# A recurrent gated network on one core: output gate's tanh apart, one agent row block on VectorE, history in single passes, new order on all engines

## What is computed

```python
def step(carry, xy):
    st, err, gs, mem, h1, c1, h2, c2 = carry
    encoded = tanh(xt @ We + st @ Ue + be)                       # 24 values
    new_state = tanh(einsum('bd,cds->bcs', xt, Wx) + einsum('bs,cst->bct', st, Ws) + bk)   # 8 candidates of 32
    mem = concatenate([[encoded, err], mem[:, :-1]])             # the last 20 entries of 25
    a = relu(mem.reshape(b, -1) @ enc_w1 + enc_b1)               # 64
    agent_in = relu(a @ enc_w2 + enc_b2)                         # 16
    h1, c1 = lstm_cell(agent_in, h1, c1)
    h2, c2 = lstm_cell(h1, h2, c2)
    gate = softmax(h2 @ gate_w + gate_b)                         # 8
    theta = clamp01(mean(abs(mem[:, :10, -1])) * 2.5)
    gate = gate * theta + gs * (1 - theta)
    st = einsum('bc,bcs->bs', gate, new_state)
    pred = clamp01(st[:, -1]);  err = pred - yt
```

## Time and profile before

| what | value |
|---|---|
| median of 3 runs | 5656.33 us (5656.32 to 5656.89) |
| profiled execution: span | 5654.1 us |
| instructions | 184300 |
| phases | 512, of 10.93 us each in the middle of the run |
| VectorE busy in the window of one phase, 2799.12 to 2810.05 us | 9.08 us |
| ScalarE busy in it | 7.48 us |
| TensorE busy in it (recorded, with the tails of matmuls) | 10.63 us |

### The profile page before, as it was taken

One profiled execution on the slowest core, in us unless ns is written; L12 is line 12 of the kernel. 1 busy time (PEld: TensorE's weight loads), 2 busy tenths in 40 slices (PEclk: granted clock), 3 DMA queues, 4 the chain that ended last, 5 costly groups with the idle time before them and its releaser, 6 DMA issues.

```text
span 5654.1 us, 184300 instructions
## 1 busy us (share of the span) xinstructions
PE 5444.6 (96%) x67584; PEld 3397.7 (60%) x67584; DVE 4678.1 (83%) x12841; ACT 3830.9 (68%) x9217; POOL 1646.7 (29%) x3589
## 2 busy tenths in 40 slices
PE   7999999999999999999999999999999999999998
PEld 4666666666666666666666666666666666666665
DVE  7888888888888888888888888888888888888887
ACT  5666666666666666666666666666666666666665
POOL 2222222222222222222222222222222222222222
PEclk9999999999999999999999999999999999999999
DMA  2111111111111111111111111111111111111111
GB/s 66 28 29 30 28 31 28 31 28 31 28 31 28 31 28 28 31 28 31 28 31 28 31 28 31 28 29 30 28 31 28 31 28 31 28 31 28 31 28 39
DMA packets 299286, 172.38 MB, mean 30 GB/s; under 512 B 156734, under 2 KB 263882, under 8 KB 298714
## 3 DMA queue, kind: packets, MB, share of 16 engines
q1 hardware_dynamic: 293568, 159.42, 10.8%
q10 hardware_dynamic: 5146, 3.66, 0.2%
HBM read 74.65 MB, written 2.10 MB: 14 GB/s over the span
## 4 chain that ended last, share of the span: by engine, by line
PE 69%; ACT 15%; DVE 12%; issue 4%; DMA 0%; POOL 0%; ACTq 0%; POOLq 0%; DVEq 0%
PE chain L412 17%; PE a_ps L374 10%; PE cand_ps L343 8%; PE cand_ps L334 8%; ACT a_sb L523 6%; PE chain L399 6%; PE a_ps L363 6%; ACT gates L548 5%; DVE cell_in L708 5%; DVE added L694 4%; PE chain L308 4%; PE a_ps L385 4%; PE chain L429 4%; PE cand_ps L329 3%; ACT tanh_c L554 3%
## 5 line engine op out<-in xcount | busy, mean ns | idle before, releaser
L363 PE MATMUL a_ps<-hist,w_hist 125*64 125x512 f16 x12288 | 1700.2, 381 | 24.9 <-DMA w_hist<-enc_table 24.9
L785 DVE TENSOR_REDUCE state<-mixed 128x64 f32<-128x512 f32 x2048 | 1352.6, 681 | 34.1 <-POOL mixed L873 0.7
L541 ACT ACTIVATE cand<-cand_ps 128x512 f32<-128x512 f32 x2048 | 1154.6, 590 | 184.8 <-PE cand_ps L343 184.8
L412 PE MATMUL chain<-cell_in,cell_w 128*64 128x128 f32 x16384 | 1092.8, 276 | 0.7 <-ACT cell_in L531 0.5
L412 PEld LDWEIGHTS chain<-cell_in,cell_w 128*64 128x64 f32 x16384 | 888.3, 136 | 288.2 <-ACT cell_in L531 181.5
L900 POOL TENSOR_TENSOR err_ring<-pred_now,ys 128x8 f32 x512 | 128.6, 251 | 3106.0 <-DVE pred_now L792 3106.0
L548 ACT ACTIVATE gates<-chain 128x512 f32<-128x512 f32 x1024 | 611.4, 597 | 619.8 <-PE chain L412 619.8
L363 PEld LDWEIGHTS a_ps<-hist,w_hist 125*64 125x64 f16 x12288 | 658.6, 110 | 447.2 <-issue 26.0
L554 ACT ACTIVATE tanh_c<-gates 128x128 f32<-128x128 f32 x1024 | 316.7, 309 | 690.0 <-DVE gates L700 690.0
L694 DVE SCALAR_TENSOR_TENSOR added<-gates 128x256 f32<-128x256 f32 x1024 | 435.5, 425 | 419.4 <-ACT gates L548 419.4
L708 DVE SCALAR_TENSOR_TENSOR cell_in<-gates,tanh_c 64x128 f32<-64x128 f32 x2048 | 588.0, 287 | 159.4 <-ACT tanh_c L554 145.6
(11 more groups left out here) (74 smaller groups left out, 6660.7 us busy)
## 6 DMA issues: line engine op xcount, KB each, us to landing
x_sb<-in_x_l SPq DMA_DIRECT2D x260, 256.0 KB, 2.8
hist<-entry_parts SPq DMA_DIRECT2D x2048, 25.0 KB
w_hist<-enc_table SPq DMA_DIRECT2D x258, 128.0 KB, 2.4
y_rows<-in_y_l SPq DMA_DIRECT2D x260, 8.0 KB
ys<-in_y ACTq DMA_DIRECT2D x1, 2048.0 KB, 16.3
preds_out<-preds SPq DMA_DIRECT2D x1, 2048.0 KB, 8.1
cand<-in_encoder ACTq DMA_DIRECT2D x1, 640.0 KB, 3.8
cell_w<-in_cell ACTq DMA_DIRECT2D x2, 256.0 KB, 4.8
```

The costliest lines, as they stand in the source:

```text
L363: nc.tensor.matmul(a_ps[g][ENC * half:ENC * half + ENC, :], w_hist[0:HROWS, w_slot(u), kk, wp, :], hist[0:HROWS, xp, k, at:at + 512], star ...
L412: last = nc.tensor.matmul(chain[g][rows, P * r:P * r + P], cell_w[c][:, hf, r, :], cell_in[c][:, g, hf, :], start=False, stop=True, skip_g ...
L541: ins = nc.scalar.activation(cand[:, g, q // 2, :, q % 2, :, :].rearrange("p h s c -> p h (s c)"), cand_ps[q][:, :].rearrange("p (h k) -> ...
L785: V.tensor_reduce(state[:, g, hf, 2 * pair:2 * pair + 2, :], mixed[:, pair, hf, :, :, :], AX, ALU.add)\
```

## The change

- The tanh of a cell's gates is cut in two: columns 128 to 511 (the three gates that the cell's value needs) and then the output gate alone, with a semaphore of its own, `q_out_gate`.
- The agent input's two instructions are shared out: ScalarE keeps one half of the rows, VectorE takes the other (`agent_input` there, semaphore `q_in_high`).
- The history product is called in pieces of one or two passes (`PIECES`), which are put between other work.
- The candidates' bias matmul leaves its place beside the candidates and goes behind the newest entry's product.
- `q_sum` and the pool's product get a semaphore for each half or tile, and waits that were together are put where each is needed; the two copies of the hidden value are separated.
- All four engines have a new order within the phase. A semaphore count is shifted where a phase now sees an item earlier or later.

```diff
-SUMS = 2
-CAND_ORDER = (2, 1, 3, 0)
-MIX_ORDER = (1, 0)
+CAND_ORDER = (1, 0, 2, 3)
+FIRST_HALF = (0, 0)
+PIECES = ((0, 0), (1, 0), (0, 1))
...
             def state_transpose(item, hf):
                 g, n, u = item
-                pe.wait_ge(q_sum[hf], SUMS * n)
+                for pair in range(2):
+                    pe.wait_ge(q_sum[hf][pair], n)
...
+            def history(item, kk, first=0, end=len(PIECES)):
                 g, n, u = item
                 k = HT - 1 - kk
-                for t, (wp, xp) in enumerate(((0, 0), (1, 0), (0, 1))):
+                for t in range(first, end):
+                    wp, xp = PIECES[t]
...
             def phase(items, extra):                      # tensor
                 new, cur, old = items
+                if old:
+                    history(old, 3, 2, 3)
+                    encoder1_now(old)
+                    candidates_bias(old)
+                if cur:
+                    history(cur, 0, 1, 2)
+                if old:
+                    bias_of_cell(old, 0)
+                    encoder2(old)
+                if cur:
+                    history(cur, 0, 2, 3)
+                    history(cur, 1, 0, 2)
+                if old:
+                    cell_gates(old, 0)
+                    candidates_x(old)
+                    candidates_s(old)
+                if cur:
+                    encoded_x(cur, extra)
+                if old:
+                    bias_of_cell(old, 1)
+                    cell_gates(old, 1)
+                if cur:
+                    history(cur, 1, 2, 3)
+                    state_transpose(cur, 0)
+                    state_transpose(cur, 1)
+                    history(cur, 2, 0, 2)
                 if old:
                     logit_bias(old)
+                if new:
+                    history_waits(new, extra)
+                    history(new, 0, 0, 1)
+                if cur:
+                    encoded_s(cur)
+                    history(cur, 2, 2, 3)
+                    history(cur, 3, 0, 2)
                 if old:
                     gate_logits(old)
...
             def cell_tanhs(item, c):
                 g, n, u = item
                 act.wait_ge(q_cps[c], n)
-                nc.scalar.activation(gates[c][:, g, 0:4, :].rearrange("p r b -> p (r b)"), chain[g][:, :],
+                nc.scalar.activation(gates[c][:, g, 1:4, :].rearrange("p r b -> p (r b)"), chain[g][:, P:4 * P],
                                      ACT.Tanh).then_inc(q_gates[c], 1)
+
+            def cell_tanh_out(item, c):
+                g, n, u = item
+                nc.scalar.activation(gates[c][:, g, 0, :], chain[g][:, 0:P], ACT.Tanh).then_inc(q_out_gate[c], 1)
...
             def phase(items, extra):                      # scalar
...
                 if new:
                     encoded(new)
                 if cur:
                     candidates(cur, 3)
+                    exponentials(cur)
                 if new:
                     entry_high(new)
                     encoder1(new)
                 if cur:
+                    next_hidden(cur, 0)
+                if new:
+                    agent_input(new, 0)
+                    cell_tanhs(new, 0)
+                if cur:
+                    next_hidden(cur, 1)
+                if new:
+                    cell_tanh_out(new, 0)
+                    value_tanh(new, 0)
+                    candidates(new, 1)
+                    candidates(new, 0)
+                    candidates(new, 2)
+                    cell_tanhs(new, 1)
+                    cell_tanh_out(new, 1)
...
+            def agent_input(item, hf):                    # vector
+                g, n, u = item
+                rows = AGENT_ROWS[hf]
+                dve.wait_ge(q_inps, n)
+                V.tensor_scalar(cell_in[0][rows, g, hf, :], a_ps[g][rows, 0:P], enc2_bias[rows, 0:1], 0.0,
+                                ALU.add, ALU.max).then_inc(q_in_high, 1)
...
             def phase(items, extra):                      # vector
...
+                    mix(cur, 0)
+                if new:
+                    agent_input(new, 1)
+                if cur:
                     mix(cur, 1)
+                    mix_sum(cur, 0, 0)
                 if new:
                     cell_terms(new, 0)
                     cell_value(new, 0)
                 if cur:
+                    mix_sum(cur, 1, 1)
+                if new:
+                    new_hidden(new, 0, 0)
+                    new_hidden(new, 0, 1)
+                    error_sum(new)
+                if cur:
+                    mix_sum(cur, 0, 1)
+                    mix_sum(cur, 1, 0)
+                    prediction(cur)
+                if new:
+                    cell_terms(new, 1)
```

More of the change, by code:

```diff
@@ L136, in recurrent_kernel @@
                                     "inps", "in", "candps"))
-        q_keptfrom, q_mulpool = (sem(f"q_{n}") for n in ("keptfrom", "mulpool"))
+        q_keptfrom = sem("q_keptfrom")
+        q_mulpool = [sem(f"q_mulpool{q}") for q in range(2)]
         q_cand = [sem(f"q_cand{q}") for q in range(Q)]
@@ L147, in recurrent_kernel @@
                                     "ring", "predout"))
-        q_sum = [sem(f"q_sum{hf}") for hf in range(HF)]
+        q_out_gate = [sem(f"q_out_gate{c}") for c in range(2)]
+        q_in_high = sem("q_in_high")
+        q_sum = [[sem(f"q_sum{hf}_{pair}") for pair in range(2)] for hf in range(HF)]
         block = ctx.enter_context(nc.Block())
@@ L298, in x_wait, with encoded_x @@
                     pe.wait_ge(s_x[x_slot(u)], extra[0][u] if extra else 16)
-            def encoded_x(item, before, extra):
+            def encoded_x(item, extra):
                 g, n, u = item
                 x_wait(item, extra)
-                if before:
-                    for pair in MIX_ORDER:
-                        pe.wait_ge(q_mul[pair], before[1] + GROUPS if pair == MIX_ORDER[1] else before[1])
+                for pair in range(2):
+                    pe.wait_ge(q_mul[pair], n)
                 for rows in ENTRY_ROWS:
@@ L320, in quarter, with candidates_bias @@
                 return t[D_IN * q:D_IN * q + D_IN]
-            def candidates_x(item, before, extra):
+            def candidates_bias(item):
                 g, n, u = item
-                if before:
-                    for q in CAND_ORDER:
-                        pe.wait_ge(q_cand[q], before[1])
+                for q in CAND_ORDER:
+                    pe.wait_ge(q_cand[q], n)
                 for q in range(Q):
@@ L524, in encoder1 @@
                     .then_inc(q_a, 1)
-            def agent_input(item):
+            def agent_input(item, hf):
                 g, n, u = item
+                rows = AGENT_ROWS[hf]
                 act.wait_ge(q_inps, n)
-                for hf in range(HF):
-                    rows = AGENT_ROWS[hf]
-                    last = nc.scalar.activation(cell_in[0][rows, g, hf, :], a_ps[g][rows, 0:P], ACT.Relu,
-                                                bias=enc2_bias[rows, 0:1])
-                last.then_inc(q_in, 1)
+                nc.scalar.activation(cell_in[0][rows, g, hf, :], a_ps[g][rows, 0:P], ACT.Relu,
+                                     bias=enc2_bias[rows, 0:1]).then_inc(q_in, 1)
             def candidates(item, q):
@@ L555, in value_tanh, with next_hidden @@
                     .then_inc(q_tanhc[c], 1)
-            def next_hidden(item):
+            def next_hidden(item, hf):
                 g, n, u = item
-                act.wait_ge(q_h[0], n)
-                for hf in range(HF):
-                    rows = CELL0_OUT[hf]
-                    last = nc.scalar.activation(cell_in[0][rows, g, hf, :], cell_in[1][rows, g, hf, :], ACT.Copy)
-                last.then_inc(q_hnext, 1)
+                rows = CELL0_OUT[hf]
+                if hf == 0:
+                    act.wait_ge(q_h[0], n)
+                last = nc.scalar.activation(cell_in[0][rows, g, hf, :], cell_in[1][rows, g, hf, :], ACT.Copy)
+                if hf == HF - 1:
+                    last.then_inc(q_hnext, 1)
             def exponentials(item):
@@ L617, in _ @@
             for hf in range(HF):
-                V.memset(state[:, :, hf, :, :], 0.0).then_inc(q_sum[hf], SUMS * GROUPS)
+                for pair in range(2):
+                    V.memset(state[:, :, hf, 2 * pair:2 * pair + 2, :], 0.0).then_inc(q_sum[hf][pair], GROUPS)
             V.memset(share[:, :, :], 0.0).then_inc(s_prep, 1)
@@ L790, in prediction @@
                 for hf in range(HF):
-                    dve.wait_ge(q_sum[hf], SUMS * n + SUMS * GROUPS)
+                    for pair in range(2):
+                        dve.wait_ge(q_sum[hf][pair], n + GROUPS)
                 V.tensor_scalar(pred_now[:, g, :].rearrange("p (a h l) -> p a h l", a=2, h=HF),
```

157 lines of the change are left out of this document (61 added, 96 removed).

## The result

The changed kernel takes 5723.15 us (median of 4 runs, 5722.94 to 5724.69) against 5656.56 us of the kernel before (4 runs). The ratio is 1.0118 [1.0104, 1.0133]. The forecast was 5446 us with a range of 5390 to 5600: wrong in sign, 277 us off. The profiled execution has a span of 5718.5 us, with a granted clock of 0.998 of the 2.4 GHz level.

The account below looks back on a forecast made before the run. TensorE was taken to bound the kernel, with 0.95 us of stalls in a 10.93 us phase. TensorE's order gave 10.47, VectorE's loop 10.52, and the later counts: 0.41 us saved over 512 phases, 210 us, giving 5446 us (range 5390 to 5600).

Parts of the forecast that it names:

- Agent rows: VectorE's half behind the new gate: takes 0.25 us (bounds 0.19 to 0.36), ready at 4.55, just under the first cell's 4.62.
- the walk: The prediction's pass through the new order of one phase, in us, with time 0 at the start of TensorE's line 315.
- VectorE's loop: VectorE from error rows to last sum: 1.10 + 8.64 + 0.17 - 0.40 = 9.51; the next phase starts at 10.52.
- Encoder: TensorE's start of phase: line 374 starts at 1.71 instead of 1.88; stalls of 0.50 shrink to 0.15 plus the slower start.
- Bias moved: Candidates' bias on TensorE behind line 374: same matmuls, two changes of shape added, done at 3.03.
- The whole drain: TensorE at a change of shape: if 0.17 instead of 0.10, three added changes cost 0.5 instead of 0.3, phase 10.7.
- Tanh apart: ScalarE's cell tanh: 384 columns take 0.50, path to the cell's value 0.10 shorter, twice; 0.42 more ScalarE work hidden.
- The one on the slower side: Agent rows late behind the softmax on VectorE, first cell waits: loss beyond 4.9; at 5.1 phase 11.15, 5769 us; chance 0.08.
- The rival that changes of shape eat half: TensorE: added changes cost a whole tail each, pieces of two matmuls start slowly; phase 10.72, 5548 us; chance 0.20.
- The rival of TensorE alone: TensorE alone bounds, no VectorE loop; agent rows as short as 0.19 and overlapping; phase 10.42, 5397 us; chance 0.07.

Follow-up runs that it names:

- low_late: The changed kernel with GpSimd's entry product moved behind its gate sum, so that it no longer runs while VectorE computes the share: 5536.52 us.

## Why the prediction was wrong

**The step that failed** is in *Agent rows*: "It stands behind the new gate, which ended at 2802.94 = 3.82, 0.3 earlier now". The softmax did start earlier, but the new gate ended at 2812.22 = 3.98, 0.16 later than before. Of that chain the share product alone grew, from 0.167 to 0.553 us, and the agent rows behind it ended at 4.96, where the walk had them ready at 4.55. The sum took every duration of the chain from the old trace, and the share product's 0.167 held only for where it stood relative to GpSimd's entry product, an overlap that the sum did not have at all. In low_late, without the hold, the new gate ends at 2806.20 - 2802.61 = 3.59, 0.23 earlier: the step is nearly right there. Of the 277 us missed, 187 are this (5723.15 - 5536.52).

The Trainium skill (SBUF — State Buffer, Who interferes with whom) says that a VectorE instruction with two SBUF inputs contends with a GpSimd instruction that reads SBUF, and that the order of issue decides which one waits. The runs agree on the first: 0.166 us with one input in PSUM against 0.553 us with two in SBUF, both begun inside the entry product. On the second they show one side: in every hold GpSimd's product had started first. I applied no such rule: "the earlier new error on GpSimd cost nothing: GpSimd works 3.2 us of 10.5" looked at how busy GpSimd is, not at what lies beside it.

**The other 90 us** (5536.52 - 5446) are sizes. The phase of low_late shown is 10.64 against 10.52 forecast, and the mean over 450 phases is 10.70; the phases are not alike, 10.63 to 10.93 between the 5th and 95th in 100. By steps:

- *Agent rows, the price:* 0.335 us, forecast 0.25, inside the bounds of 0.19 and 0.36 and near the upper end. VectorE's next product starts 0.26 behind it, where *VectorE's loop* had 0.17 for them (0.25 less 0.08); who waits for the result pays 0.335. The 0.29 of line 708 is half of the 0.59 in the earlier trace rows, not in the earlier trace rows. The 0.15 that the walk added for the second wait instruction came from no row. In low_late the rows end at 4.57, and line 417 starts at 4.67, not 4.62.
- *Line 338:* 0.97, not 0.86, behind the first cell; and that cell takes 1.02, not 0.97. The prediction read the 1.03 of line 412 as the price of a wait ahead of it, but there the six history matmuls took 0.68, so that TensorE had hardly waited. With these and 0.03 from the two lines behind, line 417's second call starts at 8.32 instead of 8.08. From there to the next phase 0.12 comes back.

**What was right.** *Encoder:* line 377 at 1.67. *Bias moved:* 330 at 2.69, 388 at 3.56, and a net gain of 55 us. The whole drain that the prediction worked out beside the Trainium skill's rule (TensorEngine Tiling (Array Packing), Key Properties) isn't seen: line 330 starts 1.02 behind line 377 in place of 0.88, a gap of 0.14, and 0.06 ahead of the recorded end of line 377. *Tanh apart:* 0.491 us for 384 columns, forecast 0.50, and 87 us gained. *VectorE's loop:* the idle piece of 0.40 went, and in low_late the last sum ends at 2812.23 - 2802.61 = 9.62, forecast 9.51; it starts with the error rows at 1.06, forecast 1.10. *Agent rows moved:* 108 us gained once the hold is gone.

**The rivals.** The one on the slower side had the second half of the mechanism: the agent rows are late, so the first cell waits. What makes them late it left open ("behind a slower product"); no row that the prediction showed pointed to it. It had a chance of 0.08. Its scale was too mild. It had a loss beyond 4.88 (4.47 + 0.41) and 11.15 at 5.1; by that, rows that end at 4.96 cost 0.08 a phase, some 5697 us (an estimate), and it was 5723. The rival that changes of shape eat half named 10.72 and 5548 us, and low_late came to 10.70 and 5537. That is luck of the number: its reason doesn't show, since line 330 starts at 2.68 to 2.69 and the next history piece 0.32 to 0.33 behind it, as the walk had them (2.69 and 0.34), and the piece of two matmuls takes 0.24, given as 0.22. The rival of TensorE alone names 5397 us, which is 5395 by its own 10.42. Between low_late (rows end at 4.57, mean phase 10.70) and the change (4.96, 11.07) the phase grows 0.37 for 0.39, so by a straight line between the two, an estimate, break-even with 10.94 lies near 4.8.

**What stays open.** Why line 338 takes 0.11 us more without the bias matmul ahead was not tried, and how the 0.12 us come back between the second cell and the next phase was not followed. That the hold comes from a read interface of SBUF that the two engines share is the account of the Trainium skill (SBUF — State Buffer, Who interferes with whom); the runs show only who waits for whom, from which operands, and until when.

## What to carry to other kernels

Before a reorder is priced with old durations, list each VectorE instruction with two SBUF inputs that can fall beside a GpSimd instruction that reads SBUF, and work out both starts, not only both lengths: here 0.23 us earlier on one and 0.21 us later on the other turned a 0.17 us product into one of 0.55. When work is moved onto an engine's chain, the chain's idle time is what had made such stalls free; count it as spent. If a hold appears, moving the GpSimd instruction beside work that has an operand in PSUM brought 187 us here; changing the operands of one product passed part of the stall to the next and brought 100.

## What was not expected of the hardware

- In the change, a VectorE product of 128x8 with two SBUF inputs stood still for 0.39 us beside a GpSimd product of 0.67 us, and ended 0.02 us behind it, in 511 of 512 phases; in the one without an entry product beside it it took 0.167 us. A 128x64 product held in the same way (0.40 us, alone 0.225) ended 0.08 us behind. In the seven kernels with a held product, taking its own time off its recorded end gives a release 0.14 to 0.15 us ahead of GpSimd's recorded end; a product begun 0.09 ahead of that end, as in the kernel before, was not held.
- With one of the two inputs in PSUM it took 0.166 us in the midst of the GpSimd product. The reduction (0.22 us) and the reciprocal (0.20), with one input, lay wholly beside the entry product in the kernel before, and took as long in low_late, where it comes later; the mix product with one input in PSUM took 0.69 us beside the entry product (low_late) and beside other GpSimd work (the change).
- GpSimd's product did not grow: 0.670 us on average, against 0.673 before.
- The held instruction is recorded as busy, not as waiting. The stall shows as a longer mean duration, and in no view of waits.
